# RWKV attention and a mixture of experts on one core: VectorE reads turned rows and counts from PSUM, and a new order between the blocks and the experts

## What is computed

```
x = x + rwkv(layernorm(x))
    rwkv: xx = previous row - row;  mixed_k = row + xx * maa_k   for k in r, k, v, g
          r, k, v = mixed @ W.T per head (16 heads of 16 channels);  g = gelu(mixed_g @ Wg.T)
          scan over chunks: y = (r k * Wmat) v + (r state) * wb;  state = ws * state + (k * wk) v
          out = (groupnorm(y) * ln_w + ln_b) * g @ Wo.T
x = x + moe(layernorm(x))
    moe: 8 experts, the best 2 of softmax(x @ gate.T) for each row;
         an expert takes the first rows that chose it, up to a capacity, counted by a cumulative sum;
         out = weight * w2(silu(w1 row) * (w3 row))
```

## Time and profile before

| what | value |
|---|---|
| median of three runs | 847.17 us |
| the profiled execution's own time | 846.3 us |
| its span, first to last instruction | 844.6 us |
| TensorE busy | 814.7 us, 96% |
| VectorE busy | 505.7 us, 60%; eight tenths and more from 42 to 317 us |
| ScalarE busy | 464.4 us, 55% |
| GpSimd busy | 468.3 us, 55% |
| mean granted TensorE clock | 0.995 of full |

### The profile page before, as it was taken

The page is one execution under the profiler, slowest core; times in us unless marked ns, Lnnn a source line. Parts: engine busy times, 40 slices in busy tenths (PEclk is TensorE's granted clock), DMA queues, the critical chain, the costliest instruction groups (busy, mean ns, idle before and its releaser), DMA issues. The chain is left out here.

```text
span 844.6 us, 17509 instructions
## 1 busy us (share of the span) xinstructions
PE 814.7 (96%) x6291; PEld 674.5 (80%) x6291; DVE 505.7 (60%) x1286; ACT 464.4 (55%) x860; POOL 468.3 (55%) x529
## 2 busy tenths in 40 slices
PE   5999999999999989899999999999999999999997
PEld 4777787777777667678998788898788899788886
DVE  6789988899998886343543543544443545353441
ACT  4478877778787667264543543644552544453331
POOL 6445577777777857475444356453436452535215
PEclk9999999999999999999999999999999999999999
DMA  5852032213111121546333334342415442413114
GB/s 163 334 209 70 28 108 68 76 52 96 40 40 48 58 91 72 178 157 135 101 70 40 110 95 70 95 113 27 124 60 79 121 106 26 95 35 44 20 14 50
DMA packets 50746, 74.30 MB, mean 88 GB/s; under 512 B 5072, under 2 KB 42448, under 8 KB 50640
## 3 DMA queue, kind: packets, MB, share of 16 engines
q1 hardware_dynamic: 35760, 53.72, 19.2%
q0 software_dynamic: 14592, 19.18, 13.6%
q10 hardware_dynamic: 288, 0.01, 0.0%
HBM read 38.67 MB, written 34.22 MB: 86 GB/s over the span
## 5 line engine op out<-in xcount | busy, mean ns | idle before, releaser
L1648 POOL DMA_INDIRECT out<-ysb,index x80 | 124.7, 1558 | 145.6 <-DVE ysb L1887 111.1
L2001 PE MATMUL p<-xh,whi 128*128 128x512 f32 (+2 forms) x504 | 185.4, 368 | 1.4 <-POOL wlo L1637 0.5
L1863 DVE TENSOR_TENSOR hid<-gated,p 128x512 f32<-128x512 f32 (+1 forms) x126 | 81.0, 643 | 176.2 <-ACT gated L1710 176.2
L2003 PE MATMUL p<-xh,wlo 128*128 128x512 f32 (+2 forms) x504 | 185.3, 368 | 0.0
L2002 PE MATMUL p<-xl,whi 128*128 128x512 f32 (+2 forms) x504 | 184.6, 366 | 0.0
L2027 PE MATMUL py<-w,hh 128*128 128x512 f32 x448 | 162.5, 403 | 4.2 <-DVE hl L1132 3.7
L1710 ACT ACTIVATE gated<-p 128x512 f32<-128x512 f32 (+1 forms) x126 | 70.8, 562 | 157.4 <-PE p L2003 152.8
L1637 POOL TENSOR_TENSOR wlo<-wraw,whi 128x448 fp32r<-128x448 f32 x56 | 70.8, 1267 | 89.8 <-ACT whi L1696 84.4
L2001 PEld LDWEIGHTS p<-xh,whi 128*128 128x128 f32 x504 | 94.7, 188 | 19.2 <-issue 3.5
L2026 PE MATMUL py<-w,hl 128*128 128x256 f32 x384 | 108.5, 283 | 0.0
L2002 PEld LDWEIGHTS p<-xl,whi 128*128 128x128 f32 x504 | 94.8, 188 | 15.2
(11 more groups left out here) (215 smaller groups left out, 1430.7 us busy)
## 6 DMA issues: line engine op xcount, KB each, us to landing
wraw<-in_w SPq DMA_DIRECT2D x24, 896.0 KB
disp<-wraw SPq DMA_DIRECT2D x16, 662.5 KB, 8.2
xtok<-disp SPq DMA_DIRECT2D x16, 530.0 KB, 4.8
x_ring<-in_x SPq DMA_DIRECT2D x16, 256.0 KB, 3.3
out<-x SPq DMA_DIRECT2D x16, 256.0 KB
xtok<-disp SPq DMA_DIRECT2D x8, 265.0 KB
out<-ysb,index POOLq DMA_INDIRECT x80
disp<-row,slot_i POOLq DMA_INDIRECT x64
```

The lines of the kernel that those rows point to most:

```text
L1648: nc.gpsimd.indirect_dma_start(out, bass.IndirectOffsetOnAxis(ap=index[e.const % 2][:, t:t + 1], axis=0), ysb[j % NY][:], None, compute_op ...
L1863: nc.vector.tensor_tensor(hid[k][:, 0:w], gated[k][:, 0:w], p3[k][:, 0:w], ALU.mult).then_inc(hid_ready, 1)
L2001: nc.tensor.matmul(dst[:, 0:w], hi[m][:, wcut], xh[xcut], start=(kt == 0), stop=False)
L2003: ins = nc.tensor.matmul(dst[:, 0:w], lo[m][:, wcut], xh[xcut], start=False, stop=(kt == KT - 1))
```

## The change

Five things are edited.

1. `shifted` and `mixing` on VectorE take the unshifted rows from pX in PSUM in place of xT in SBUF (the shifted ones still come from xT). So pX must stay until k = 0, 1, 2 are mixed: `project_o` gets three waits for it, and `mixing(c + 1, 2)` moves on VectorE from behind `stats1` to the head of a turn of the loop.
2. `slots` multiplies the counts by took first and in place in PSUM, in place of the places later in SBUF. `count` waits for `slots` of the block before.
3. The last block's gating is done by VectorE (`gated_last(15)`) and no longer by GpSimd.
4. GpSimd's list behind the loop is new: `norm2` stands between the two tiles of a scatter, `weight_low(11)` behind `scatter(14)`.
5. VectorE's, ScalarE's and TensorE's lists behind the loop are new in places.

```diff
@@ on_gpsimd, behind the loop
-        scatter(12)
+        scatter(12, range(0, 1))
+        norm2(14)
+        scatter(12, range(1, TPS))
         chain.reset()
-        norm2(14)
-        gated(15)
-        scatter(13)
+        scatter(13, range(0, 1))
+        norm2(15)
+        scatter(13, range(1, TPS))
         chain.reset()
         early_index()
-        norm2(15)
+        scatter(14)
         weight_low(11)
-        scatter(14)
@@ on_scalar, behind the loop
         early_hidden_hi(2)
+        logit_exp(15)
         early_gate(3)
         early_hidden_hi(3)
-        logit_exp(15)
@@ on_vector
-                nc.vector.tensor_tensor(diff[:], xt[:, :, 0:W], xt[:, :, 1:], ALU.subtract).then_inc(diff_ready, 1)
+                nc.vector.tensor_tensor(diff[:], xt[:, :, 0:W], pX[:], ALU.subtract).then_inc(diff_ready, 1)
...
-                                                         xT[b % 2][:, c, 1:], ALU.mult, ALU.add)
+                                                         pX[:, c, :], ALU.mult, ALU.add)
...
+        def gated_last(b):
+            dve.wait_ge(z_ready, b + 1)
+            dve.wait_ge(gT_ready, b + 1)
+            wait(dve, wo_done, b)
+            nc.vector.tensor_tensor(zg[:], z[:], gT[b % 2][:], ALU.mult).then_inc(zg_ready, 1)
...
+                chain.link(nc.vector.tensor_tensor(p_count, p_count, took[r][:], ALU.mult))
                 chain.link(nc.vector.tensor_tensor(over[:], p_count, limit[:].unsqueeze(1).to_broadcast([P, TPS, E]), ALU.is_gt))
...
-                chain.link(nc.vector.tensor_tensor(slotf[:], slotf[:], took[r][:], ALU.mult))
...
             mixing(c + 1, 1)
+            mixing(c + 1, 2)
...
-            mixing(c + 1, 2)
@@ on_vector, behind the loop
-        slots(12)
-        chain.reset()
         residual(14)
         logit_sum(14)
         early_lo(0)
+        slots(12)
+        chain.reset()
         early_lo(1)
         logit_max(14)
         stats2(14)
+        normed_y(15)
         slots(13)
         chain.reset()
-        normed_y(15)
+        gated_last(15)
         best_two(14)
         tally(14)
         early_hidden(0)
         residual(15)
         logit_sum(15)
+        logit_max(15)
         early_hidden(1)
-        logit_max(15)
         stats2(15)
-        chain.reset()
         early_hidden_lo(0)
         early_hidden_lo(1)
-        early_hidden(2)
         slots(14)
         chain.reset()
+        early_hidden(2)
         early_weight()
         early_hidden_lo(2)
+        best_two(15)
+        tally(15)
         early_hidden(3)
         early_hidden_lo(3)
-        best_two(15)
-        tally(15)
@@ on_tensor
 def project_o
                 pe.wait_ge(xT_ready, min(b + 3, STEPS))
+                for k in range(3):
+                    pe.wait_ge(mixed_ready[k], min(b + 3, STEPS))
 def count
                 pe.wait_ge(took_ready, b + 1)
+                wait(pe, slot_ready, b)
@@ on_tensor, behind the loop
         group_sums(15)
+        early_up(0)
         count(13)
-        early_up(0)
         early_up(1)
```

## The result

The changed kernel takes 854.67 us (median of 4 runs, 854.34 to 856.17) against 846.90 us beside it: 1.0099 of before, interval 1.0084 to 1.0114. The forecast was 845.3 us, the range 842.8 to 849.4. It is outside, on the slower side. The profiled execution took 854.9 us (span 852.0).

What follows compares the result with a forecast made beforehand. TensorE's 18.02 us floor bounds the blocks, plus 0.37 us per late block waiting for VectorE, held by GpSimd. -2.6 + 0.1 + 0.6 = -1.9 us on 846.3 gives 844.4, in the runs' median 845.3 us; range 842.8 to 849.4.

Steps and rivals of the forecast that it cites:

- diff and mixing from PSUM: VectorE in the blocks: unblocked mixings take 0.40 us each, 0.35 us goes; GpSimd's two L586 gain as much.
- mixing(.., 2) moved ahead: VectorE's loop: third mixing adds 0.80 us ahead of yn, mostly repaid; first mask +0.1 us, bounds -0.3 to +0.8.
- What this moves on GpSimd: Late blocks: zg and wlo come 0.94 us later, L1075 goes first unblocked, -0.43 us; net -2.6 us over 8 blocks.
- the slower rival: Late blocks: wlo still first, blocking L1075 0.85 us; loop 18.9 us, kernel 851.9, or 849.4 if alternating; chance 0.17.
- The alternation that I granted: Within the wlo-first rival: a late block moves wlo back behind L1075, halving the price to 849.4 us.
- 0.45 us in 11 blocks: PSUM-cost rival (chance 0.05) at the skill's 65 ns per VectorE operation: 0.45 us per block, 849.7 us.
- slots: VectorE's product with took moved to the front, into PSUM: gain 0 to 0.2 us, value 0.
- the waits of `project_o` and `count`: TensorE's added waits: count's already met; project_o's three cost 0 to 2 us over 14 blocks, value 0.
- Behind the blocks: Tail: 2.5 us pause before early_up(5), no wait before project_o(15), restart +0.6 us, bounds -0.7 to +1.5.
- the rival of a second fall of the clock: Tail: the new 2.5 us TensorE pause brings another clock fall, +1.7 us, 847.0 us; chance 0.2.

Runs made afterwards that it cites:

- 0.9979: Kernel before with diff and the first two mixings reading PSUM, third mixing in its old place, GpSimd's order and tail as before: 0.9979 of before.
- 0.9993: Kernel at 0.9979 with the changed kernel's tail, but logit_exp(15), best_two(15) and tally(15) left behind early_hidden_lo(3): 0.9993 of before.
- 1.0019: Kernel before, blocks untouched, with the changed kernel's order behind the blocks and last gating by VectorE: 1.0019 of before, 847.52 us.
- 1.0055: Changed kernel with GpSimd's weight_low issued before the second tile of the scatter, behind decayed_r: 1.0055 of before, 850.41 us.
- 1.0037: Changed kernel with GpSimd's block order gated, weight_low, decayed_r, scatter, and weight_low(11) ahead of scatter(14): 1.0037 of before.
- 1.0027: Changed kernel with GpSimd's order in the blocks made gated, weight_low, decayed_r, then both tiles of the scatter: 1.0027 of before.
- 1.0013: Kernel at 0.9979 with GpSimd's weight_low directly behind gated, ahead of the first tile of the scatter: 1.0013 of before.
- 0.9982: Kernel at 0.9993 with early_hidden(2) ahead of slots(14) on VectorE, weight_low(11) still behind scatter(14): 0.9982 of before.
- 1.0076: Changed kernel's blocks with the order behind the blocks as before on all four engines, last gating by GpSimd: 1.0076 of before, 852.17 us.
- 1.0168: Kernel before with only the third mixing moved, directly behind the second and ahead of yn, all sources in SBUF: 1.0168 of before.
- 0.9978: Kernel at 0.9979 with only the last gating moved to VectorE, normed_y(15) ahead of slots(13), gated_last(15) behind it: 0.9978 of before.

## Why the prediction was wrong

- *diff and mixing from PSUM*: right. 0.40 us each, L586 1.86 us. In the old place of the third mixing it is worth 0.21% (0.9979).
- *mixing(.., 2) moved ahead*: right for the stretch it was worked out for: first mask +0.1 us behind `diff`.
- ***What this moves on GpSimd*: the step that failed**, in its two halves. `zg` was put 0.94 us later. It came 0.66 us later (5.57 against 4.91 us behind `diff`), because before the change `z` did not wait for `yn` alone: ScalarE was still at `xn`. And "L1075 then goes first and takes 0.18" did not come true: L1083 did go first, by 0.04 us, and was held 1.05 us. (The forecast had it 0.24 us ahead; no trace has the product more than 0.06 us ahead, so what such a lead would do is not shown for it.) In place of -0.43 us in the loop stands +0.6. With the +0.1 that makes 18.39 + 0.7 = 19.1 us; measured 19.05. The gain was also counted in 8 blocks, while the kernel before holds the product in six of them (0.61 to 0.66 us) and reads 0.18 us in two.
- Of the miss of 9.4 us, this term makes about 7.0 (forecast -2.6, measured +4.4 in the late blocks), the stretch from the sixteenth `turn1` to `scores_a(15)` 1.6, the tail 1.4 (forecast +0.6, measured +2.0); the rest nearly cancels.
- So the slower rival came true, with its place, its mechanism and nearly its size (18.9 us). It had 0.17, for "a delay corrects itself". Here it doesn't: `zg` isn't what TensorE waits for at `project_o` (the last mask is), so VectorE's turn and GpSimd's turn keep a fixed distance and meet every time: of the eight products from 148 to 281 us six read 1.22 to 1.23 us, and the two that `wlo` precedes by 0.3 us read 0.91 and 0.88. The alternation that I granted was not seen in this kernel; the one at 0.9993 has it, with periods of 18.50, 18.02, 18.52, 18.21, 18.49, 18.03 and 18.49 us. Its price in the forecast was also added up wrongly: half of 4.1 and the tail's 0.6 give 849.8 us, not 849.4, and 0.45 us in 11 blocks give 850.2 us, not 849.7. Neither changes where the measured time lies.
- *slots*, the waits of `project_o` and `count`: nothing, right; the two blocks of 18.03 us without `wlo` stayed at 18.03.
- *Behind the blocks*: the pause of 2.5 us (2.43), no wait before `project_o(15)`, `early_up(0)` +0.4 (+0.35), all right. The restart was +1.98 instead of +0.6 us: the rival of a second fall of the clock (0.2) came, TensorE taking 4.8 us for the slice from 339.50 to 344.31 that was forecast at 3.2. A fall came with that pause in the traces of the changed kernel and of the ones at 1.0019, 1.0055 and 1.0037 (pauses of 2.43 to 2.65 us), and not in the one at 1.0027 (2.42 us), so it is likely there and not certain.
- *From the sixteenth `turn1` to `scores_a(15)`* (the stretch around block 14 of the expectations), the +1.56 of the table: it was in no term of the forecast. The stretch took 19.6 to 23.4 us from kernel to kernel. In eleven of the seventeen traces TensorE stands still there once, for 2.8 to 4.4 us, and the timeline of the kernel at 1.0027 has the chain:

```profile
281.12 0.97 POOL L610 DMA_INDIRECT disp<-row,slot_i  x1 [0.30 <-issue]
...
284.37 0.68 ACT L744 ACTIVATE lexp<-logit,nbias,rstd 128x8 f32<-128x8 f32 x2 [4.37 <-POOL nbias L567]
...
287.10 3.33 PE L1257 MATMUL pB<-mixed,w_in_sb 128*128 128x256 f32 x7 [3.63 <-ACT gT L805]
```

  TensorE waits for ScalarE's `gT`, which stands behind `logit_exp`, which waited for GpSimd's `nbias`; and GpSimd was at four more indirect DMAs, the last at 281.12, because in this turn the loop has a second scatter (`if c >= TAIL - 2: scatter(c - 3)`), before the change and after. In the other six traces, those of before and of the changed kernel among them, ScalarE waits for `nbias` too (3.17 and 4.01 us), but TensorE stands in several pieces of 0.3 to 1.2 us with "issue" as the releaser; that part is open. The clock fell there in ten of the eleven traces and in the changed kernel's (0.52 in the window from 289.00 above), and not in the one of before. No run moved the second scatter.
- *Left open* is the +0.74 in the experts; no run was for it.

## What to carry to other kernels

When an edit shifts one engine by a fraction of a microsecond, list every instruction of VectorE with both sources in SBUF, and every cast and `tensor_scalar` in SBUF, beside every large GpSimd operation, in the new order, and give a meeting its full price even where VectorE's would start a little ahead. Then place the GpSimd operation where VectorE idles: that turned 19.06 us into 18.13 us a block with nothing else changed. No instruction with a source in PSUM was held here; move such reads, but not the instruction out of idle time that hid it. And when a hold has been moved, look for where it went: four of these experiments (1.0055, 1.0013, 0.9982, 1.0037) found it on another instruction.

## What the runs showed of the hardware

The 16-element product of VectorE was held for 1.03 to 1.08 us in all 18 cases (changed kernel, 1.0076, 1.0168) in which its record starts 0.01 to 0.06 us ahead of GpSimd's subtraction. Held were, between their shortest and longest records: products of two SBUF tiles (16 elements: 0.18 to 1.25 us), the cast of 4 elements from SBUF to SBUF (0.17 to 0.80), the `tensor_scalar` of 8 elements `limit<-base` (0.17 to 1.54), `state` (0.23 to 1.32), `mixed` from SBUF (0.45 to 1.56), `yn` (0.68 to 1.59), `hl` (0.66 to 2.07). Not held were the masks (671 to 693 ns, 128 in each trace) and the mixings from PSUM (468 to 481 ns), MAX8 (0.14 to 0.17), and `row<-lexp,lrec` beside GpSimd's issue of indirect DMAs (0.18 us). The cast and `limit<-base`, though, read up to 0.41 and 0.44 us beside such an issue alone. For the instructions with two sources in SBUF this agrees with the Trainium skill, "SBUF — State Buffer", section "Who interferes with whom", by which such an instruction contends with a GpSimd one that reads SBUF, the shared ports being an exclusive lock. By the same section the one that issues first has the pair; the 0.01 to 0.06 us by which the product's record starts first here did not save it, while a cast 0.04 us ahead of the same subtraction read its 0.17 us (at 327.21 in the kernel at 0.9978). So a lead of that size in the records is nothing to plan with.

The hold is mutual: L586 takes 2.22 us beside mixings from SBUF and 1.86 beside those from PSUM. The Trainium skill, "VectorE: DVE Perf Modes", section on the TRN2 errata, would charge PSUM sources about 65 ns more, as an estimate; the medians of 680 against 681 ns for `diff` and 477 against 476 for the mixings, with one of two sources in PSUM, show none.
